# Sorting the experts by size on the chip, and converting six of the eight experts' weights piece by piece between the expert blocks

## The chip, the cores and the metric

The kernel runs on one core of a Trainium2 chip. The metric is the time of one execution in microseconds, measured on the device; the median of several runs counts. The core's engines are TensorE (PE in the profile; PEld is its weight load), VectorE (DVE), ScalarE (ACT), GpSimd (POOL) and SyncE (SP, which here only issues DMAs; SPq is its queue).

## The reference

x is (8, 512, 256) in float32, so 4096 tokens of 256 numbers. Every product is computed in split form, three float16 products for one float32 product.

```python
xn = layernorm(x)
# s: gated linear recurrence over the 512 steps of each of 8 sequences
q, v = xn @ Wq, xn @ Wv
state[t] = sigmoid(beta) * state[t-1] + v[t]
s = (layernorm(q * state) * ln_g + ln_b) * silu(xn @ Wg) @ Wo
# g: mixture of 8 experts, two per token
logits = xn @ router.T
top_vals, top_idx = top_k(logits, 2);  gates = softmax(top_vals)
for e in range(8):
    a, b = split(xn @ w_in[e].T)          # 512 hidden each
    acc += gates[:, e] * ((silu(a) * b) @ w_out[e].T)
out = x + s * silu(acc + bias)
```

## The kernel before

**Stages.** First x is loaded, normalized, transposed and routed in 8 chunks (one sequence of 512 tokens each). VectorE works out for each token its two experts, its slot in each expert's region of `slots_dram`, and the table of blocks. Then the recurrence runs over the 8 chunks (`recur` on each engine). Beside it GpSimd scatters the 4096 rows twice into `slots_dram` (64 indirect DMAs, line 534; in chunk c after its rstd, 9, 9, 8, 8, 8, 8 of them from chunk 0 on, after 14 at the start). Then comes the expert stage: 39 blocks. The slots of each expert are cut into pairs of 128-row tiles (up to 32 blocks of 256 rows) and odd tiles (7 blocks of 128 rows, run as blocks 28 to 34). Blocks 0 and 1 are written out, blocks 2 to 25 are a loop over two blocks. At the end the summed expert outputs are read back, passed through SiLU, multiplied by s and added to x.

**The recurrence, chunk by chunk.** VectorE scans (line 1008, two instructions), converts weights (line 1017), multiplies by q (line 1021, which waits for TensorE's projection into `bankB`), multiplies by the gate and splits the chunk before (lines 1060, 1066), takes statistics (1038, 1045) and hands mean and variance over (1049, 1050). GpSimd makes rstd from them (498, 499), then does that chunk's scatters; its queue is in order, so the rstd of the next chunk stands behind them. ScalarE rescales (737), TensorE transposes, projects and so on. The order is that of the code on every engine.

**The weights.** The expert weights (8 experts, 3072 columns each per partition) come as float32 and are kept as two float16 parts, `w_hi` and `w_lo`. They are loaded in 24 pieces of 1024 columns through four buffers `wst`. ScalarE writes the high part (line 709, `convert_w`), VectorE the low part (line 1017), which frees the buffer (`w_lo_ready`), and SP loads the next (line 358). Before, four pieces are converted in each of six chunks of the recurrence, and TensorE's first expert block waits for all 24.

**A block of the expert stage.** SP loads the slots and transposes them by DMA (line 405) one block ahead. TensorE computes the hidden layer into `bankA` and `bankB` (24 matmuls each) and then the outputs of the block before into `bankD` (24). ScalarE takes SiLU (759) and the high part (764), VectorE the product (1086) and the low part (1090), each twice per block, and VectorE the gating (1107). GpSimd prepares gates and targets (559 to 597) and adds the two tiles to `y_dram` with indirect DMAs (608); each block's wait for those of the block before to have landed. Two loads of x for the end (line 433) go out after every second block from block 2 on, seven in all; they are written into the part of `work` that also holds `wst`.

**Names.** `n_pair` and `n_odd` are the pairs and odd tiles of each expert, `blk_row` and `blk_off` a block's first row and its weights' offset, `blk_e` its expert. `step(...)` on VectorE is an instruction with a wait for its own end behind it. `FIRST_ONE` is 28, the first odd block.

## Time and profile before

| | |
|---|---|
| median of 3 runs | 490.76 us (490.18 to 490.99) |
| the profiled execution | 489.02 us, its span 487.3 us |
| mean granted TensorE clock over the span | 0.956 |
| TensorE matmul busy | 408.5 us, 84% of the span |
| VectorE, ScalarE, GpSimd busy | 300.3, 215.1 and 286.4 us |
| chain that ended last | PE 58%, DVE 15%, issue 9%, POOL 7%, DMA 7%, ACT 3% |

The span goes from the first to the last instruction of the core. The chain that ended last is followed back from the last instruction, at each step to what released it; "issue" is time in which an engine waited for nothing that the profile shows.

### The profile page before, as it was taken

How to read it: one execution, taken by the hardware profiler on the slowest of the kernel's cores; microseconds unless marked ns; L12 is line 12 of the kernel's file. 1: busy time of each engine (PE TensorE's matmuls, PEld its weight loads, DVE VectorE, ACT ScalarE, POOL GpSimd, SP SyncE). 2: the span in 40 equal slices, each digit the busy share in tenths (PEclk: the TensorE clock that was granted, in tenths of full speed). 3: DMA queues.
4: the chain of work that ended last, by engine and by line, in shares of the span. 5: the costliest groups of instructions: out<-in, count | busy, mean ns of one | idle time of the engine just before them, and what ended most of it. 6: DMA issues, size and time to landing. Idle time of an engine off the chain costs nothing.

```text
span 487.3 us, 11896 instructions
## 1 busy us (share of the span) xinstructions
PE 408.5 (84%) x3304; PEld 324.8 (67%) x3305; DVE 300.3 (62%) x602; ACT 215.1 (44%) x340; POOL 286.4 (59%) x504
## 2 busy tenths in 40 slices
PE   1757784999986999999999999999999999899000
PEld 1544352665653898888888888888888755788000
DVE  4898999999985355454554545464554544444056
ACT  3882363787756554334343434333342333332051
POOL 4725777678870325675775666666575743366532
PEclk9999899899999999999999999999999999999655
DMA  8893274567963259888766655666655455663498
GB/s 259 277 350 133 98 253 132 191 236 256 318 212 86 56 77 191 189 169 140 128 99 115 87 108 87 109 96 109 104 81 87 64 99 93 119 65 34 86 333 356
DMA packets 90810, 74.07 MB, mean 152 GB/s; under 512 B 52880, under 2 KB 82576, under 8 KB 90768
## 3 DMA queue, kind: packets, MB, share of 16 engines
q1 hardware_dynamic: 75824, 54.86, 41.9%
q0 software_dynamic: 13296, 17.83, 21.8%
q10 hardware_dynamic: 1664, 1.06, 0.7%
q8 instruction: 13, 0.21, 0.2%
q14 instruction: 13, 0.11, 0.1%
HBM read 40.00 MB, written 28.74 MB: 141 GB/s over the span
## 4 chain that ended last, share of the span: by engine, by line
PE 58%; DVE 15%; issue 9%; POOL 7%; DMA 7%; ACT 3%; SPq 1%; DVEq 0%; POOLq 0%; ACTq 0%
PE bankA L1181 19%; PE bankB L1181 19%; PE bankD L1181 17%; POOL slots_dram L534 4%; DMA w_raw<-x_in 2%; PE bankC L1181 2%; DMA y_dram<-rows_raw 2%; DVE w_raw L1017 1%; POOL stat L498 1%; DVE work L1008 1%; DVE bn L1038 1%; DMA w_raw<-y_dram 1%; DVE w_raw L1166 1%; DVE bn L833 1%; DVE work L1021 1%
## 5 line engine op out<-in xcount | busy, mean ns | idle before, releaser
L608 POOL DMA_INDIRECT y_dram<-rows_raw x64 | 103.3, 1614 | 27.2 <-issue 27.2
L1181 PE MATMUL bankD<-w_raw,rows_raw 128*128 x852 | 99.5, 273 | 0.3 <-DVE rows_raw L1090 0.3
L534 POOL DMA_INDIRECT slots_dram<-rows_raw,pos_i x64 | 74.2, 1159 | 30.9 <-issue 20.0
L1181 PEld LDWEIGHTS bankD<-w_raw,rows_raw 128*128 128x128 f16 x852 | 83.0, 98 | 12.0 <-issue 0.7
L1181 PE MATMUL bankA<-rows_raw,w_raw 128*128 128x256 f16 x768 | 89.1, 273 | 1.3 <-DMA rows_raw<-rows_raw 1.3
L1181 PE MATMUL bankB<-rows_raw,w_raw 128*128 128x256 f16 x768 | 89.1, 273 | 0.0
L1181 PEld LDWEIGHTS bankA<-rows_raw,w_raw 128*128 x768 | 74.8, 98 | 10.6 <-issue 1.9
L1181 PEld LDWEIGHTS bankB<-rows_raw,w_raw 128*128 x768 | 75.1, 98 | 8.7
L1090 DVE TENSOR_TENSOR rows_raw<-rows_raw 128x512 f16<-128x512 f32 x64 | 44.4, 694 | 45.5 <-ACT rows_raw L764 45.5
L1086 DVE SCALAR_TENSOR_TENSOR rows_raw<-rows_raw,bankA 128x512 f32<-128x512 f32 x32 | 22.0, 687 | 77.4 <-ACT rows_raw L759 75.1
L764 ACT ACTIVATE rows_raw<-rows_raw 128x512 f16<-128x512 f32 x64 | 40.3, 630 | 51.5 <-DVE rows_raw L1086 51.5
L759 ACT ACTIVATE rows_raw<-bankA 128x512 f32<-128x512 f32 x32 | 19.1, 596 | 96.1 <-PE bankA L1181 80.0
L605 POOL TENSOR_TENSOR rows_raw<-spare 128x1 f32<-128x1 f32 x32 | 6.2, 193 | 50.0 <-DVE rows_raw L1107 23.2
L1107 DVE TENSOR_SCALAR rows_raw<-bankD,rows_raw 128x256 f32<-128x256 f32 x64 | 27.9, 478 | 3.2 <-PE bankD L1181 3.2
L559 POOL TENSOR_TENSOR rows_raw<-rows_raw,blk_e 128x2 f32<-128x2 f32 x32 | 19.8, 618 | 13.9 <-DMA rows_raw<-slots_dram 13.9
L1017 DVE SCALAR_TENSOR_TENSOR w_raw<-work,w_raw 128x1024 f32 (+1 forms) x24 | 27.6, 1212 | 0.0
L1071 DVE TENSOR_TENSOR rows_raw<-rows_raw 128x512 f16<-128x512 f32 (+1 forms) x39 | 24.8, 636 | 3.2 <-ACT rows_raw L748 3.2
L737 ACT ACTIVATE work<-bankD,stat 128x256 f32<-128x256 f32 x32 | 15.4, 562 | 23.8 <-POOL stat L499 23.8
L498 POOL TENSOR_TENSOR stat<-stat,neg_half 128x4 f32<-128x4 f32 x16 | 16.9, 1054 | 15.0 <-DVE stat L1050 14.3
L608 POOL DMA_INDIRECT y_dram<-work,rows_raw x7 | 11.6, 1658 | 23.4 <-DMA y_dram<-work,rows_raw 12.9
L1181 PE MATMUL bankC<-wat_hi,work 128*128 128x256 f16 x128 | 23.8, 284 | 1.1 <-ACT work L730 1.1
L748 ACT ACTIVATE rows_raw<-rows_raw 128x512 f16<-128x512 f32 (+1 forms) x39 | 22.5, 577 | 2.6 <-DMA rows_raw<-slots_dram 2.6
(182 smaller groups left out, 638.7 us busy)
## 6 DMA issues: line engine op xcount, KB each, us to landing
work<-w_exp_in SPq DMA_DIRECT2D x24, 512.0 KB, 5.3
rows_raw<-slots_dram SPq DMA_DIRECT2D x32, 256.0 KB
w_raw<-x_in SPq DMA_DIRECT2D x9, 512.0 KB, 4.5
y_dram<-bias_in SPq DMA_DIRECT2D x4, 1024.0 KB, 12.3
w_raw<-y_dram SPq DMA_DIRECT2D x8, 512.0 KB, 7.2
out<-w_raw SPq DMA_DIRECT2D x8, 512.0 KB, 4.9
work<-x_in SPq DMA_DIRECT2D x7, 512.0 KB
slots_dram<-fill SPq DMA_DIRECT2D x9, 260.0 KB, 6.0
```

The source lines that it names most:

```text
L498: step(pool.tensor_tensor(stat[i][:, 1, :], stat[i][:, 0, :], neg_half[:, :], ALU.pow))
L534: pool.indirect_dma_start(out=slots_dram, out_offset=bass.IndirectOffsetOnAxis(slot, 0), in_=row, in_offset=None, bounds_check=SLOTS - 1, ...
L559: pool.tensor_tensor(is_first[i][:, :], meta_in[i][:, :, 0], e_b, ALU.subtract)\
L608: pool.indirect_dma_start(out=y_dram, out_offset=bass.IndirectOffsetOnAxis(to, 0), in_=ones_y[:, b - FIRST_ONE, :] if ones else ys[i][:, s ...
L748: act.activation(split16[i][:, 0:units(b), 0, :], slot_in[i][:, 0:units(b), :], ACT.Copy)\
L764: act.activation(g_hi[i][:, 2 * j:2 * j + 2, 0:n], g32[j][:, :, 0:n], ACT.Copy)\
L1017: dve.scalar_tensor_tensor(w_lo[:, piece], wst[:, i % STAGES, :], WSCALE, w_hi[:, piece], ALU.mult, ALU.subtract).then_inc(w_lo_ready, 1)
L1071: dve.tensor_tensor(split16[i][:, 0:units(b), 1, :], slot_in[i][:, 0:units(b), :], split16[i][:, 0:units(b), 0, :], ALU.subtract).then_inc ...
L1086: dve.scalar_tensor_tensor(g32[j][:, :, 0:n], sil[j][:, :, 0:n], 1.0 / WSCALE, AB[j][:, :, BLOCK:BLOCK + n], ALU.mult, ALU.mult).then_inc( ...
L1090: dve.tensor_tensor(g_lo[i][:, 2 * j:2 * j + 2, 0:n], g32[j][:, :, 0:n], g_hi[i][:, 2 * j:2 * j + 2, 0:n], ALU.subtract).then_inc(g_split, 1)
L1107: last = dve.tensor_scalar(ones_y[:, n, :] if ones else ys[i][:, s, :], bankD[:, i, s * D:s * D + D], gates[:, s:s + 1], None, ALU.mult)
L1181: last = pe.matmul(out_ap, lhsT, rhs, start=(n == 0), stop=(n == len(todo) - 1))
```

## The change

The experts are sorted by their number of pairs, largest first, on VectorE (`sort_experts`, called in the first chunk of the recurrence), and the table of blocks is built over the sorted experts. The weights are loaded in the sorted order: a piece's place in DRAM is read from a table (`piece_of`), a third of an expert per piece. Six pieces (two experts) are converted in the recurrence, one per chunk: ScalarE in chunks 1 to 6, VectorE in chunks 2 to 7. The other 18 are converted one per block, in blocks 0 to 17. TensorE waits for three pieces before block 0 and for b + 3 before block b. The loads of x are split: three after blocks 2 to 4, four after blocks 26 to 29. The loops of VectorE, ScalarE and SP over the chunks, and SP's over blocks 2 to 17, are written out; the expert blocks 2 to 17 are a loop over four blocks on VectorE and ScalarE.

```diff
-W_CHUNKS = CH - 2
-PIECES = 4
-PIECE = E * EW // (W_CHUNKS * PIECES)
+PER_EXPERT = 3
+PIECE = EW // PER_EXPERT
+PIECES = E * PER_EXPERT
+EARLY_PIECES = 6
+LAST_PIECE_BLOCK = PIECES - EARLY_PIECES
+X_FIRST = 3
+ID_STEP = 4096
...
 # SP
-            load_w(0)
+            def load_w(p):
+                if p >= STAGES:
+                    sp.wait_ge(w_lo_ready, p + 1 - STAGES)
+                piece = sp.value_load(piece_of[0:1, p:p + 1], min_val=0, max_val=PIECES - 1)
+                sp.dma_start(wst[:, p % STAGES, :], w_exp_v[:, bass.ds(piece, 1), :].rearrange(
+                    "p a w -> p (a w)")).then_inc(wst_loaded[p % STAGES], 16)
...
-            for c in range(1, 3):
-                load_w(c)
-
-            with sp.Fori(3, W_CHUNKS) as c:
-                load_w(c)
+            sp.wait_ge(experts_sorted, 1)
+            for p in range(STAGES):
+                load_w(p)
...
+            for p in range(STAGES, EARLY_PIECES + 3):
+                load_w(p)
 
             sp.wait_ge(pads_filled, 16 * (E + 1))
             sp.wait_ge(rows_scattered, 16 * N_SCATTERS)
...
+            for b in range(2, LAST_PIECE_BLOCK):
+                next_slots(b, b % 2)
+                if b + EARLY_PIECES + 1 < PIECES:
+                    load_w(b + EARLY_PIECES + 1)
+                if b == 2:
+                    sp.wait_ge(o_ps, CH)
+                if b - 2 < X_FIRST:
+                    load_x(b - 2)
...
+            with sp.Fori(LAST_PIECE_BLOCK, FIRST_ONE - 3, 2) as b:
+                next_slots(b, 0)
+                next_slots(b + 1, 1)
+            sp.wait_ge(w_lo_ready, PIECES)
             for b in range(FIRST_ONE - 2, BLOCKS):
                 next_slots(b, b % 2)
+                if X_FIRST <= b - FIRST_ONE + 2 + X_FIRST < X_EARLY:
+                    load_x(b - FIRST_ONE + 2 + X_FIRST)
 # ScalarE, in the recurrence
-                for i in range(PIECES if convert else 0):
-                    convert_w(c, i)
+                if 1 <= c <= EARLY_PIECES:
+                    convert_w(c - 1, (c - 1) % STAGES)
 # ScalarE, in the expert stage
+            with act.Fori(2, LAST_PIECE_BLOCK - 3, STAGES) as b:
+                for j in range(STAGES):
+                    halves(b + j, j % 2, 2)
+                    convert_w(b + (EARLY_PIECES + j), j)
 # VectorE
+            def sort_experts():
+                step(dve.scalar_tensor_tensor(key[:, :], n_pair[:, 0:E], float(E), ids, ALU.mult, ALU.subtract))
+                step(dve.tensor_tensor(beats[:, :, :], in_columns(key[:, :]), in_rows(key[:, :]), ALU.is_gt))
+                step(dve.tensor_reduce(rank[:, :], beats[:, :, :], AX.X, ALU.add))
+                step(dve.tensor_tensor(is_rank[:, :, :], in_rows(ids), in_columns(rank[:, :]), ALU.is_equal))
+                step(dve.tensor_tensor(by_rank[:, :, :], is_rank[:, :, :], in_columns(ids), ALU.mult))
+                step(dve.tensor_reduce(order[:, 0:E], by_rank[:, :, :], AX.X, ALU.add))
...
+            def low_w(p, stage):
+                dve.wait_ge(w_hi_ready, p + 1)
+                piece = bass.ds(p * PIECE, PIECE)
+                dve.scalar_tensor_tensor(w_lo[:, piece], wst[:, stage, :], WSCALE, w_hi[:, piece],
+                                         ALU.mult, ALU.subtract).then_inc(w_lo_ready, 1)
...
-                for i in range(PIECES if convert else 0):
-                    dve.wait_ge(w_hi_ready, (c - 1) * PIECES + (i + 1))
-                    piece = bass.ds(((c - 1) * PIECES + i) * PIECE, PIECE)
-                    dve.scalar_tensor_tensor(w_lo[:, piece], wst[:, i % STAGES, :], WSCALE, w_hi[:, piece],
-                                             ALU.mult, ALU.subtract).then_inc(w_lo_ready, 1)
+                if 2 <= c <= EARLY_PIECES + 1:
+                    low_w(c - 2, (c - 2) % STAGES)
...
+            with dve.Fori(2, LAST_PIECE_BLOCK - 3, STAGES) as b:
+                for j in range(STAGES):
+                    halves(b + j, j % 2)
+                    gate_y(b + (j - 1), 1 - j % 2, False)
+                    low_w(b + (EARLY_PIECES + j), j)
 # TensorE
-                pe.wait_ge(w_lo_ready, W_CHUNKS * PIECES)
+                pe.wait_ge(w_lo_ready, PER_EXPERT)
...
-            with pe.Fori(2, FIRST_ONE - 3, 2) as b:
+            with pe.Fori(2, LAST_PIECE_BLOCK + 3, 2) as b:
+                for j in range(2):
+                    pe.wait_ge(w_lo_ready, b + (j + PER_EXPERT))
+                    one_block(b + j, j)
+            pe.wait_ge(w_lo_ready, PIECES)
+            with pe.Fori(LAST_PIECE_BLOCK + 4, FIRST_ONE - 3, 2) as b:
                 one_block(b, 0)
                 one_block(b + 1, 1)
```

In the listings below a row is the line of the kernel, the operation, the tile written, those read, and the size; xN stands for N in a row. An ISA row sets or waits. Lines of the changed kernel differ: 1059 is the conversion (1017 before), 1079 the product with q (1021), 1069 the scan (1008), 414 the transposes (405), 394 the load of slots (385), 367 the load of weights (358), 434 that of x (433).

On VectorE, first chunk of the recurrence, between the counting of blocks and the product with q (`bankB`) there stood:

```order
L938 SCALAR_TENSOR_TENSOR w_raw<-w_raw 128x8
L940 SCALAR_TENSOR_TENSOR w_raw<-w_raw 128x8
L942 SCALAR_TENSOR_TENSOR w_raw<-w_raw 128x8
L1021 SCALAR_TENSOR_TENSOR work<-bankB,work 128x1024
L898 TENSOR_TENSOR w_raw<-w_raw 128x128
```

In the changed kernel the sorting (lines 960 to 974) stands behind the first of these rows, ahead of the two scans and the product:

```order
L960 SCALAR_TENSOR_TENSOR w_raw<-w_raw 128x8
L961 TENSOR_TENSOR w_raw<-w_raw 128x64
L962 TENSOR_REDUCE w_raw<-w_raw 128x8
L963 TENSOR_TENSOR w_raw<-w_raw 128x64
L964 TENSOR_TENSOR w_raw<-w_raw 128x64
L965 TENSOR_REDUCE w_raw<-w_raw 128x8
L966 SCALAR_TENSOR_TENSOR piece_of<-w_raw 1x24
L971 TENSOR_TENSOR w_raw<-w_raw 128x64
L972 TENSOR_TENSOR w_raw<-w_raw 128x64
L973 TENSOR_REDUCE w_raw<-w_raw 128x8
L974 TENSOR_REDUCE w_raw<-w_raw 128x8
L987 SCALAR_TENSOR_TENSOR w_raw<-w_raw 128x8
```

So 11 instructions more stand ahead of the product with q, the positions of the second half of the rows, and the first chunk's statistics.

On VectorE, one of the chunks 2 to 6, from the scan to the product with q, before:

```order
L1008 SCALAR_TENSOR_TENSOR work<-cols,bankA 128x512 x2
L1015 ISA
L1017 ISA
L1017 SCALAR_TENSOR_TENSOR w_raw<-work,w_raw 128x1024
L1015 REGISTER_ALU
L1017 ISA
L1017 SCALAR_TENSOR_TENSOR w_raw<-work,w_raw 128x1024
L1015 REGISTER_ALU
L1017 ISA
L1017 SCALAR_TENSOR_TENSOR w_raw<-work,w_raw 128x1024
```

A fourth conversion and then the product follow there. The same chunk now:

```order
L1069 SCALAR_TENSOR_TENSOR work<-cols,bankA 128x512 x2
L1059 SCALAR_TENSOR_TENSOR w_raw<-work,w_raw 128x1024
L1079 SCALAR_TENSOR_TENSOR work<-bankB,work 128x1024
L1118 TENSOR_TENSOR work<-work 128x512 x2
L1124 TENSOR_TENSOR work<-work 128x512 x2
```

One conversion is left between the scans and the product.

On SP, from the transposes of block 2 on, before:

```order
L405 DMA_TRANSPOSE rows_raw<-rows_raw 128x4x128 x2
L384 TENSOR_LOAD blk_row
L384 ISA x2
L385 ISA
L385 DMA rows_raw<-slots_dram 128x2x256
L405 DMA_TRANSPOSE rows_raw<-rows_raw 128x4x128 x2
L391 TENSOR_LOAD blk_row
L391 ISA x2
L392 ISA
L392 DMA rows_raw<-slots_dram 128x2x4
L433 DMA work<-x_in 128x1024 x2
```

And in the changed kernel:

```order
L414 DMA_TRANSPOSE rows_raw<-rows_raw 128x4x128 x2
L366 TENSOR_LOAD piece_of
L366 ISA x2
L367 ISA
L367 DMA work<-w_exp_in 128x1024
L434 DMA work<-x_in 128x1024
L393 TENSOR_LOAD blk_row
L393 ISA x2
L394 ISA
L394 DMA rows_raw<-slots_dram 128x2x256
L414 DMA_TRANSPOSE rows_raw<-rows_raw 128x4x128 x2
```

A load of weights and a load of x (behind a wait for the last output projection) now stand ahead of the slots of block 5 and the transposes of block 3.

## Rows read from the trace of the kernel before

**Rows 1.** Chain that ended last: start us, us, what, merged over like pieces

```profile
144.70 3.34 DMA slots_dram<-rows_raw,pos_i
...
161.85 2.62 PE bankA L1181 x24
...
186.42 2.62 PE bankA L1181 x24
...
194.28 2.62 PE bankA L1181 x24
```

**Rows 2.** Order of time, GpSimd, recurrence: start, us, instruction [idle before <-released by]

```profile
58.61 1.05 POOL L498 TENSOR_TENSOR stat<-stat,neg_half 128x4 f32<-128x4 f32 x1
...
73.73 1.05 POOL L498 TENSOR_TENSOR stat<-stat,neg_half 128x4 f32<-128x4 f32 x1
...
90.63 1.04 POOL L498 TENSOR_TENSOR stat<-stat,neg_half 128x4 f32<-128x4 f32 x1 [1.93 <-DVE stat L1050]
...
95.81 1.98 POOL L534 DMA_INDIRECT slots_dram<-rows_raw,pos_i  x1 [0.30 <-issue]
98.09 0.97 POOL L534 DMA_INDIRECT slots_dram<-rows_raw,pos_i  x1 [0.30 <-issue]
...
104.60 1.06 POOL L498 TENSOR_TENSOR stat<-stat,neg_half 128x4 f32<-128x4 f32 x1
...
118.69 1.06 POOL L498 TENSOR_TENSOR stat<-stat,neg_half 128x4 f32<-128x4 f32 x1
...
132.76 1.24 POOL L498 TENSOR_TENSOR stat<-stat,neg_half 128x4 f32<-128x4 f32 x1
...
145.69 1.05 POOL L498 TENSOR_TENSOR stat<-stat,neg_half 128x4 f32<-128x4 f32 x1
```

**Rows 3.** Order of time, VectorE and ScalarE, recurrence

```profile
44.60 0.29 DVE L875 TENSOR_TENSOR w_raw<-w_raw 128x128 f32<-128x128 f32 x1
...
51.79 0.17 DVE L938 SCALAR_TENSOR_TENSOR w_raw<-w_raw 128x8 f32<-128x8 f32 x1
52.00 0.17 DVE L940 TENSOR_TENSOR_SCAN w_raw<-w_raw 128x8 f32<-128x8 f32 x1
...
57.74 0.16 DVE L1050 TENSOR_SCALAR stat<-mv 128x4 f32<-128x4 f32 x1
...
70.31 0.15 DVE L1050 TENSOR_SCALAR stat<-mv 128x4 f32<-128x4 f32 x1
...
93.46 4.60 DVE L1017 SCALAR_TENSOR_TENSOR w_raw<-work,w_raw 128x1024 f32 x4
...
101.88 3.89 ACT L709 ACTIVATE w_raw<-work 128x1024 f32 x4
```

**Rows 4.** Order of time, TensorE, recurrence: query projections of two chunks

```profile
93.63 0.59 PE L1181 MATMUL bankB<-xs_raw,wat_hi 128*128 x2
...
105.77 0.59 PE L1181 MATMUL bankB<-xs_raw,wat_hi 128*128 x2
```

**Rows 5.** Order of time, four engines, expert stage

```profile
178.89 2.52 SPq L405 DMA_TRANSPOSE rows_raw<-rows_raw  x2
...
197.02 0.60 ACT L759 ACTIVATE rows_raw<-bankA 128x512 f32<-128x512 f32 x1 [3.29 <-PE bankA L1181]
...
197.65 0.69 DVE L1086 SCALAR_TENSOR_TENSOR rows_raw<-rows_raw,bankA 128x512 f32<-128x512 f32 x1 [2.35 <-ACT rows_raw L759]
...
205.65 1.59 POOL L608 DMA_INDIRECT y_dram<-rows_raw  x1 [0.52 <-issue]
...
212.90 0.19 POOL L605 TENSOR_TENSOR rows_raw<-spare 128x1 f32<-128x1 f32 x1 [1.31 <-DMA y_dram<-rows_raw]
...
222.26 1.60 POOL L608 DMA_INDIRECT y_dram<-rows_raw  x1 [0.52 <-issue]
```

**Rows 6.** Stretches: busy per engine, granted clock, DMA share, GB/s

```profile
core 0: us, PE busy (x) PEld busy (x) DVE busy (x) ACT busy (x) POOL busy (x), PEclk, DMA share, GB/s
181.00:189.00 8.00, 8.00 (x76) 6.96 (x74) 4.09 (x7) 2.94 (x5) 3.75 (x12) 1.00 1.24 212
162.00:382.00 220.00, 220.00 (x2017) 197.16 (x2016) 114.44 (x195) 86.95 (x148) 137.38 (x300) 1.00 0.66 112
```

113 lines of the change are left out of this document (64 added, 49 removed).

## The prediction, made before the changed kernel ran

> **What bounds the kernel now.** I read the chain of waits first, then one engine at a time in order of time, then the busy time in stretches.
>
> The kernel has three stretches. From about 162 us to 382 us TensorE runs without a gap at a granted clock of 1.00, the higher level of 2.4 GHz [rows 6]; nothing that an engine beside it does there costs anything until TensorE has to wait for it. The end behind that stretch (the blocks of one tile, the last blocks, the sum and the store) keeps its instructions. So the change can gain only before 162 us, and lose after it.
>
> Before 162 us the chain runs, from about 90 us on, through GpSimd: its scatters of token rows stand on the chain until the last one (issued at 144.70, landed at 148.04), then the loads of the first slots, and at 161.85 the first expert block begins [rows 1]. GpSimd's queue holds, for each chunk, the four small instructions for rstd and then eight or nine scatters. The starts of L498 give its pace: 58.61, 73.73, 90.63, 104.60, 118.69, 132.76, 145.69 [rows 2]. The three chunks from 90.63 to 132.76 take 42.13, so 14.04 each. GpSimd waits there once, 1.93 us before 90.63, for VectorE's variance [rows 2]; otherwise it is its own bound. Its scatters don't all cost the same: one takes 0.97 us at 98.09, but 1.98 us at 95.81, and the latter lies in the 4.60 us of VectorE's four conversions at 93.46 [rows 2, 3]. At 98.09, when the conversions have just ended and their loads are still in flight, the scatter is fast again, so I take VectorE and not the DMA traffic for the cause. The price per chunk: the scatters between two L498 take 14.04 us with four conversions in the way, and 12.93 us in the last such chunk (132.76 to 145.69) [rows 2], over which only the tail of the conversions falls.
>
> TensorE has its own floor in this stretch: from the query projection of one chunk (93.63) to that of the next (105.77) it runs without a gap, 12.14 us [rows 4].
>
> **The change part by part.**
>
> Sorting the experts puts 11 VectorE instructions ahead of the product and of the positions of the second half. A step of 8 elements per partition costs 0.21 us from start to start (51.79 to 52.00), one of 128 elements is busy for 0.29 us, so 0.33 with the same gap [rows 3]. Most of the new ones have 64 elements and waits behind them: between the two, taken as 0.26; one has 8 elements, two are not waited for. 8 x 0.26 + 0.21 + 2 x 0.15 = 2.6 us. (All at the lower bound 2.3, all at the upper 3.6.) They delay the first variance, whose last instruction starts at 57.74 and ends at 57.90, to 60.5. GpSimd's first rstd started at 58.61, behind 14 scatters [rows 2, 3], and now waits: **+1.9 us** on GpSimd.
>
> The conversions: before, VectorE has four of them in each of six chunks; now one in each of six (chunks 2 to 7, none in chunk 1). For GpSimd, chunk 1 took 73.73 - 58.61 = 15.12; I take off 1.6 for the conversions that no longer hold its scatters (two scatters of nearly 2 us in place of two of 0.97, less a little), which gives rstd 1 at 60.5 + 13.5 = 74.0, where it was. The next chunk worked until 90.63 - 1.93 = 88.70; with one conversion instead of four I take off 1.1, so it is done at 87.9. VectorE decides now: variance 1, whose last instruction started at 70.31, comes 0.5 later (behind GpSimd's later rstd 0, through the rescaling, the transposes and the statistics), the table of blocks has six instructions more at 0.12 to 0.26 (+1.4), and three conversions less in chunk 2 save 3 x 4.60/4 = 3.4 us [rows 3]. So rstd 2 moves from 90.63 to 90.63 + 0.6 + 1.4 - 3.4 = 89.2: **-1.4 us**.
>
> From there three chunks run at GpSimd's pace again. With one conversion per chunk the row that is nearest is the chunk of 12.93 us; 12.9 each, against 14.04, is 3 x 1.1 = **-3.4 us**. The bounds are nothing (the scatters stay slow, rival 1) and TensorE's 12.14, which would give 3 x 1.9 = 5.7. The last chunk changes nothing: its conversions hardly met it. One conversion in VectorE's chunk 7 lies ahead of a wait for TensorE and costs nothing; the path there goes over the scatters' landing and the slots [rows 1].
>
> Here the Trainium skill speaks against my reading of the scatters. SBUF — State Buffer, section Who interferes with whom, says that a VectorE instruction with two SBUF inputs holds up only GpSimd instructions that read SBUF, and infers that writing DMA descriptors needs the other interface, so that such an instruction would not slow a scatter. By that rule the slow scatters have another cause and the -3.4 falls away; this case's rows (1.98 against 0.97 us) point the other way.
>
> In the expert stage ScalarE gets one more conversion per block (3.89 us for four in the trace [rows 3], so 1.0 each) and VectorE one of 1.15, for 18 pieces. In a block of 7.86 us (186.42 to 194.28 [rows 1]) ScalarE stands idle 3.29 us before its first SiLU (197.02) and VectorE 2.35 us before its first product (197.65) [rows 5]. The new instructions are written behind the last use of each engine's block, so they fall into these gaps: 0 us, as long as the piece has landed. If the gap were gone, each would cost up to 1.2 us per block. The weight loads: 15 more (blocks 2 to 16), 512 KB each, one block ahead and more of their conversion. DMA is busy 0.66 of the stretch 162 to 382, and reached 1.24 where two loads of x are in flight (181 to 189), without a wait of TensorE [rows 6]. TensorE's own new waits (block b for b + 3 pieces) are met three blocks early: VectorE has converted b + 6 by the end of block b.
>
> One place is tight. SP used to issue the transposes of block 3 from 178.89 on [rows 5], ahead of any load of x; now a weight load, the wait for the last output projection (which ends where block 2 begins, one block ahead of 186.42, so about 178.5) and a load of x stand ahead of them. They are needed at 186.4, when block 3 begins, 7.5 us after 178.89 [rows 1]. I put **+0.3 us** here, between nothing and 1.5. The loads of x 3 to 6 come at blocks 26 to 29, one per block, and end long before the sum needs them: 0.
>
> Sum: -1.4 - 3.4 + 0.3 = -4.5 us (the +1.9 is inside the -1.4). The profiled execution takes 489.02 (span 487.3), so 484.5; it lies 1.74 below the median of the runs, so that the median goes from 490.76 to **486.3 us**. The bounds of the terms alone (sort 2.3 to 3.6, pace 12.14 to 13.3, block 3 nothing to 1.5) give 483.5 to 488.5.
>
> **The rivals.**
>
> 1. The scatters stay slow for a reason that isn't VectorE. Then rstd 1 comes at 60.5 + 15.1 = 75.6 and rstd 2 at 75.6 + 14.96 = 90.6, where it was, and all chunks keep 14.04: 490.8 plus 0.3. For it: the page above. Against it: the scatters at 95.81 and 98.09. Chance 0.07.
>
> 2. TensorE becomes the bound of the recurrence, because single conversions fall beside the rstd instructions and delay no scatter: 12.14 per chunk, 486.3 - 2.3 = 484.0. For it: the variance is ready about 2.5 us before GpSimd comes to it, so the conversion lies about there. Chance 0.12.
>
> 3. The chain of scatter-adds falls behind in the expert stage. Each block's needs the one before it landed; with loads of x in flight two pairs after 205.65 the next starts at 222.26, 8.3 us for each over a block's 7.86, and at 212.90 GpSimd is seen behind a wait of 1.31 us for the landing [rows 5]. So a block under load adds 0.44 of lag. Lag is paid only when VectorE's gating waits for the scatters of two blocks back: they may take 15.7 us and take 7.2 (205.65 to 212.90), so from 8.5 us of lag on. 15 blocks at 0.44 give 6.6; with conversions beside the scatters' start it could pass 8.5. If it bites: 1 to 3 us, so 488.5. Chance 0.07.
>
> 4. Slower: the DMA engines become the bound of the 15 blocks with loads. Per block they are busy 0.66 x 7.86 = 5.2 us, so 2.7 are spare. The stretch from 181 to 189 has the base of 5.3 and 1.24 x 8 = 9.9 in all, so two loads of x and their neighbours took 4.6, or 2.3 each: below 2.7, but not far. From 2.7 us a load the transposes come late in each block. At 3.3 a load: 15 x 0.6 = 9 us lost, 486.3 + 9 = 495. Chance 0.09.
>
> **How the numbers follow.** My forecast (484.8 to 488.4) has 0.65; with rival 2 and rival 3 nine tenths of what is left ends faster too. A change of 0.2%, about 1 us, is what a measurement of this kernel can tell from none. Faster by over 0.2%: 0.65 + 0.12 + 0.06 = 0.83. Within: 0.07 + 0.01 = 0.08. Slower: 0.09. The range 483.3 to 490.0 leaves out rivals 1 and 4 and a little of rival 2, under 2 in 10.
>
> **What would show each step.** In the changed profile: GpSimd's L498 of the recurrence first at about 60.5 and with a wait for VectorE, then at 74, 89.2, 102, 115, 128; scatters of about 1.9 us nearly gone; the first block of TensorE at about 157.4; TensorE busy all of the 220 us behind it; the idle times of ScalarE and VectorE in a block down to about 2.2 and 1.2. It is wrong if the paces stay at 14 us, if TensorE shows a wait for a transpose or for a conversion in blocks 2 to 17, or if the time from the first block to the end grows.

## The result and the profile after

| | before | changed |
|---|---|---|
| median | 490.61 us (490.18 to 490.99, 4 runs) | 483.22 us (482.23 to 484.36, 4 runs) |
| ratio of the times, 95% interval | | 0.985 (0.9826 to 0.9875) |
| profiled execution, span | 489.02, 487.3 us | 484.36, 482.6 us |
| start of the first expert block | 161.85 us | 153.27 us |
| from there to the end of the span | 325.5 us | 329.3 us |

Faster, by 7.4 us where 4.5 were forecast; 483.22 lies just below the range. The lead at the first expert block is even larger, 8.6 us, and 3.9 us of it are gone again at the end of this profiled execution. Two more sets of the changed kernel gave 481.78 and 482.22 us (below).

GpSimd in order of time, the starts of the recurrence's rstd (L511 is what L498 was; answers to [rows 2]):

```profile
60.66 1.04 POOL L511 TENSOR_TENSOR stat<-stat,neg_half 128x4 f32<-128x4 f32 x1 [1.91 <-DVE stat L1108]
...
74.01 1.06 POOL L511 TENSOR_TENSOR stat<-stat,neg_half 128x4 f32<-128x4 f32 x1
...
88.89 1.04 POOL L511 TENSOR_TENSOR stat<-stat,neg_half 128x4 f32<-128x4 f32 x1 [0.16 <-DVE stat L1108]
...
102.48 1.04 POOL L511 TENSOR_TENSOR stat<-stat,neg_half 128x4 f32<-128x4 f32 x1 [0.66 <-DVE stat L1108]
...
115.24 1.05 POOL L511 TENSOR_TENSOR stat<-stat,neg_half 128x4 f32<-128x4 f32 x1
...
127.39 1.06 POOL L511 TENSOR_TENSOR stat<-stat,neg_half 128x4 f32<-128x4 f32 x1
...
139.52 1.06 POOL L511 TENSOR_TENSOR stat<-stat,neg_half 128x4 f32<-128x4 f32 x1
```

The first start waits 1.91 us for VectorE's variance. The distances are 13.35, 14.88, 13.59, 12.76, 12.15 and 12.13 us; before they were 15.12, 16.90, 13.97, 14.09, 14.07 and 12.93 [rows 2].

VectorE in order of time (answers to [rows 3]): the sort lies between the first two rows, then one conversion (L1059) of a later chunk and the product behind it:

```profile
52.15 0.17 DVE L960 SCALAR_TENSOR_TENSOR w_raw<-w_raw 128x8 f32<-128x8 f32 x1
...
54.62 0.17 DVE L987 TENSOR_TENSOR_SCAN w_raw<-w_raw 128x8 f32<-128x8 f32 x1
...
117.19 1.20 DVE L1059 SCALAR_TENSOR_TENSOR w_raw<-work,w_raw 128x1024 f16<-128x1024 f32 x1
...
120.15 1.23 DVE L1079 SCALAR_TENSOR_TENSOR work<-bankB,work 128x1024 f32<-128x1024 f32 x1 [1.76 <-PE bankB L1243]
```

VectorE waits 1.76 us for TensorE behind its conversion, and TensorE has no gap through these two chunks:

```profile
115.20:139.50 24.30, 24.30 (x155) 15.94 (x153) 18.72 (x39) 14.79 (x22) 18.77 (x21) 1.00 0.38 132
```

The first three numbers are the length of the stretch, TensorE's busy time in it and its count of instructions. So TensorE bounds these chunks, at the 12.14 us that its own gapless stretch showed before [rows 4].

The chain of waits, from the last scatter to the first expert blocks, and in the tail (answers to [rows 1]):

```profile
138.53 2.48 DMA slots_dram<-rows_raw,pos_i
142.97 3.15 DMA rows_raw<-slots_dram
146.68 0.77 ACT work L709
...
150.46 2.81 PE bankC L1243 x24
153.27 2.62 PE bankA L1243 x24
...
395.22 5.06 DMA rows_raw<-rows_raw
...
410.45 6.42 DMA y_dram<-work,rows_raw
...
428.36 3.78 DMA y_dram<-work,rows_raw
...
454.54 3.90 DMA y_dram<-rows_raw
```

This splits the 8.6 us. The last scatter is issued 6.17 us earlier (138.53 against 144.70), and lands after 2.48 us in place of 3.34, which gives 0.86. The third part is the output projection behind the last chunk, 24 matmuls, which took 2.81 us here and 4.41 before (157.44 to 161.85), 1.60. In the profile before, its stretch from 157 to 161.5 us has a mean granted clock of 0.62, partly the lower level (1.2 GHz); the stretch from 150 to 153.3 of the changed kernel has 1.00 (2.4 GHz). The stretch before (the clock is the third number from the end):

```profile
157.00:161.50 4.50, 4.06 (x23) 3.04 (x24) 2.14 (x12) 1.21 (x3) 1.20 (x2) 0.62 0.50 112
```

Busy time in stretches of the changed kernel (answers to [rows 6]):

```profile
core 0: us, PE busy (x) PEld busy (x) DVE busy (x) ACT busy (x) POOL busy (x), PEclk, DMA share, GB/s
150.00:153.30 3.30, 2.84 (x26) 2.82 (x27) 2.17 (x12) 0.41 (x1) 0.91 (x1) 1.00 0.39 80
174.00:222.00 48.00, 47.84 (x437) 42.19 (x436) 31.29 (x48) 23.74 (x37) 32.24 (x65) 1.00 1.14 197
222.00:374.00 152.00, 152.00 (x1395) 136.24 (x1394) 90.56 (x146) 67.20 (x109) 107.77 (x212) 1.00 0.79 134
```

The expert stage holds: TensorE is busy 47.84 of 48 us with the DMA share up at 1.14, and all of the 152 us behind. But each block's scatter-adds into y now start later. I call lag the time from the end of the gating on VectorE (L1162, L1107 before) to the block's first scatter-add on GpSimd: 3.4 to 6 us here in blocks 1 to 26; before, it is 0.8 to 3.4 us, and only 0.8 to 1.8 from block 8 on. Two groups of the page show the same:

```profile
L572 POOL TENSOR_TENSOR rows_raw<-rows_raw,blk_e 128x2 f32<-128x2 f32 x32 | 29.4, 919 | 5.9 <-DMA rows_raw<-slots_dram 5.9
...
L1162 DVE TENSOR_SCALAR rows_raw<-bankD,rows_raw 128x256 f32<-128x256 f32 x64 | 27.9, 478 | 5.3 <-DMA y_dram<-rows_raw 3.1
```

GpSimd's destination rows take 919 ns in the mean, 618 before. From 410 us on the tail's chain in this profile is almost wholly scatter-adds and their landings, and the gating waits for them, 1.26 us at 427.07 and more at 445.40:

```profile
445.40 0.88 DVE L1162 TENSOR_SCALAR rows_raw<-bankD,rows_raw 128x256 f32<-128x256 f32 x2 [3.08 <-DMA y_dram<-rows_raw]
```

The last scatter-add is issued 4.6 us ahead of before (454.54, 459.09 before), where the lead had been 8.1 us when the blocks of one tile began (374.81 against 382.92). In neither profile of before nor in the two repeats of the changed kernel below does the gating wait for a scatter-add: there TensorE's blocks are the chain up to the last ones.

### The profile page after: what moved, and what is told of

It is laid out like the page before. It is cut to its first block, busy times and chain, and to the rows that moved or that the text cites. A ratio compares the mean times of both kernels' runs of the same rounds, so it can differ in the third digit from the quotient of the medians.

```text
span 482.6 us, 11903 instructions
## 1 busy us (share of the span) xinstructions
PE 409.0 (85%) x3304; PEld 325.9 (68%) x3305; DVE 304.8 (63%) x619; ACT 215.3 (45%) x340; POOL 288.7 (60%) x504
## 4 chain that ended last, share of the span: by engine, by line
PE 57%; DMA 12%; DVE 12%; issue 9%; POOL 6%; ACT 2%; SPq 1%; DVEq 0%; POOLq 0%; ACTq 0%
PE bankA L1243 18%; PE bankB L1243 18%; PE bankD L1243 15%; DMA y_dram<-work,rows_raw 4%; POOL slots_dram L547 3%; DMA y_dram<-rows_raw 3%; PE bankC L1243 3%; DMA w_raw<-x_in 2%; PE bankD L1342 1%; POOL stat L511 1%; DMA rows_raw<-rows_raw 1%; DMA w_raw<-y_dram 1%; DVE work L1069 1%; DVE bn L852 1%; DVE w_raw L1228 1%
## 5 line engine op out<-in xcount | busy, mean ns | idle before, releaser
L621 POOL DMA_INDIRECT y_dram<-rows_raw x64 | 109.3, 1707 | 24.6 <-issue 23.6
L547 POOL DMA_INDIRECT slots_dram<-rows_raw,pos_i x64 | 67.3, 1052 | 31.2 <-issue 20.6
L618 POOL TENSOR_TENSOR rows_raw<-spare 128x1 f32<-128x1 f32 x32 | 9.3, 289 | 51.0 <-DMA y_dram<-rows_raw 39.4
L572 POOL TENSOR_TENSOR rows_raw<-rows_raw,blk_e 128x2 f32<-128x2 f32 x32 | 29.4, 919 | 5.9 <-DMA rows_raw<-slots_dram 5.9
L1162 DVE TENSOR_SCALAR rows_raw<-bankD,rows_raw 128x256 f32<-128x256 f32 x64 | 27.9, 478 | 5.3 <-DMA y_dram<-rows_raw 3.1
L1059 DVE SCALAR_TENSOR_TENSOR w_raw<-work,w_raw 128x1024 f32 (+1 forms) x24 | 29.1, 1210 | 0.7 <-ACT w_raw L723 0.7
L511 POOL TENSOR_TENSOR stat<-stat,neg_half 128x4 f32<-128x4 f32 x16 | 16.7, 1041 | 15.0 <-DVE stat L1108 14.3
L723 ACT ACTIVATE w_raw<-work 128x1024 f32 (+1 forms) x24 | 25.0, 1042 | 0.0
```

What stands on the lines that cost most here:

```text
L547: pool.indirect_dma_start(out=slots_dram, out_offset=bass.IndirectOffsetOnAxis(slot, 0), in_=row, in_offset=None, bounds_check=SLOTS - 1, ...
L572: pool.tensor_tensor(is_first[i][:, :], meta_in[i][:, :, 0], e_b, ALU.subtract)\
L621: pool.indirect_dma_start(out=y_dram, out_offset=bass.IndirectOffsetOnAxis(to, 0), in_=ones_y[:, b - FIRST_ONE, :] if ones else ys[i][:, s ...
L723: act.activation(w_hi[:, bass.ds(p * PIECE, PIECE)], wst[:, stage, :], ACT.Copy, scale=WSCALE)\
L1059: dve.scalar_tensor_tensor(w_lo[:, piece], wst[:, stage, :], WSCALE, w_hi[:, piece], ALU.mult, ALU.subtract).then_inc(w_lo_ready, 1)
L1162: last = dve.tensor_scalar(ones_y[:, n, :] if ones else ys[i][:, s, :], bankD[:, i, s * D:s * D + D], gates[:, s:s + 1], None, ALU.mult)
```

## The experiments

Ratios are to the kernel before, run on the same chip in turns, with 95% intervals; the times of one set shouldn't be compared closer than about 1 us with those of another.

**1. The changed kernel again, twice.**

> The changed kernel a second time, for another profile and for a comparison on the chip of the next three. Open are two parts of its gain that I had not forecast: the first block began 8.6 us earlier instead of 4.8, of which 1.6 us is a projection ahead of it that ran at a granted clock of 0.5 before and at 1.0 after; and 3.4 us were given back behind block 28. If the clock part is chance, this profile may show the projection slow again (4.4 us instead of 2.8); if it belongs to the change, it is fast again. If the loss behind block 28 belongs to the change, the scatter-adds are again about 6 us behind the gating at block 27 and bind the end; if it was chance, the lag is under 3 us. Time 482 to 484.5 us.

> The changed kernel again, beside the next one on the same chip. Theory 1, the output projection at the higher clock belongs to its shorter wait of TensorE ahead of it: the 24 matmuls take 2.81 us again, and the time is 481.5 to 483.5. Theory 2, chance: 4.4 now and then.

481.78 us, ratio 0.9818 (0.9778 to 0.9857), and 482.22 us, 0.9824 (0.9799 to 0.9848). The projection took 2.81 us in both. Starts of rstd at 74.48, 90.50 and 103.55 in the first, then 12.12 to 12.15 apart. The first block began at 153.55 and 152.18, but the rest of the span took 325.65 us in one and 328.12 in the other. So what lies behind the first block varies by 3.7 us among three executions of one kernel, and the first profile was its worst. The lag was 2.5 to 5.3 us in blocks 1 to 26 of the first repeat and 1.9 to 4.0 in the second, and the second took longer behind its first block. In the second repeat TensorE waits at the heads of blocks 3 and 4 for transposes:

```profile
177.22 2.79 PE L1243 MATMUL bankA<-rows_raw,w_raw 128*128 128x256 f16 x24 [0.51 <-DMA rows_raw<-rows_raw]
...
186.39 2.79 PE L1243 MATMUL bankA<-rows_raw,w_raw 128*128 128x256 f16 x24 [1.14 <-DMA rows_raw<-rows_raw]
```

1.65 us in sum; 0.9 in the other repeat, about 0.2 in the first profile (TensorE is busy 47.84 of 48 us from 174 to 222). The recurrence varies too, up to rstd 2 (88.89, 90.50 and, in the second repeat, 89.04).

**2. Before again.**

> The kernel before, once more, for a second profile of it. In the first the output projection behind the last chunk (157.44 to 161.85, 24 matmuls) ran at a granted clock of 0.66 and took 4.41 us, 2.81 in every other profile so far. Theory 1: chance; it takes 2.8 here, and the first expert block is at 160.2. Theory 2: it belongs to that kernel (TensorE idles longer in each chunk there), and the 4.4 comes again, which would be 1.6 us of the gain. The pace of the chunks stays 14.0.

489.76 us, ratio 1.0005 (0.9979 to 1.0031). The slow projection came again, 4.42 us from 157.32 on. TensorE in order of time, the transposes and the first matmul behind them:

```profile
155.11 1.06 PE L1280 MATMUL bankD<-ident,work 128*128 128x128 f32 x8 [2.30 <-ACT work L696]
157.32 0.40 PE L1181 MATMUL bankC<-wat_hi,work 128*128 128x256 f16 x1 [1.15 <-ACT work L730]
```

and in the changed kernel's first profile:

```profile
148.25 1.06 PE L1342 MATMUL bankD<-ident,work 128*128 128x128 f32 x8 [0.41 <-ACT work L709]
150.46 0.30 PE L1243 MATMUL bankC<-wat_hi,work 128*128 128x256 f16 x1 [1.15 <-ACT work L744]
```

The waits of TensorE ahead of those transposes differ: 2.51 and 2.30 us in the two profiles of before, 0.25 to 0.52 in the three of the changed kernel. Experiments 3, 5 and 6 have more on it.

**3. What the sort costs.** Before, with the sort alone, its results unused:

```diff
@@ def count_blocks():
                                               ALU.mult, ALU.add))
+                sort_experts()
                 step(dve.tensor_tensor_scan(pair_end[:, :], ...
```

> The kernel before with the 11 instructions of the sorting added at their place in the first chunk, their results unused, the list of blocks and the conversions as before. My theory: VectorE has no idle time up to the variance of chunk 2, so the 2.6 us show in full there; the first rstd moves from 58.6 to 60.6, the third from 90.6 to about 93.2, and the kernel takes 2.6 us more than before (0.5%). Rival: GpSimd's wait of 1.9 us ahead of the third rstd takes it up, and the kernel takes 0 to 0.7 us more.

493.08 us, ratio 1.0046 (1.0016 to 1.0077): 2.7 us slower than before on the same chip (490.38). GpSimd's first and third rstd:

```profile
60.68 1.04 POOL L502 TENSOR_TENSOR stat<-stat,neg_half 128x4 f32<-128x4 f32 x1 [1.91 <-DVE stat L1082]
...
94.45 1.04 POOL L502 TENSOR_TENSOR stat<-stat,neg_half 128x4 f32<-128x4 f32 x1 [3.32 <-DVE stat L1082]
```

With four conversions per chunk in place nothing in the recurrence absorbs the sort: rstd 2 comes 3.8 us later than in the profile before. The first block comes only 2.4 us later (164.22), because the output projection took 2.81 us in this profile, after a wait of TensorE of 2.22 us ahead of the transposes. So the fast projection can also come at the old pace of 14.09 us.

**4. VectorE or the DMA traffic?** Before, without 20 of its 24 weight loads, all conversions kept (they convert the first four pieces again and again):

```diff
@@ sync engine
-            for c in range(1, 3):
-                load_w(c)
-            with sp.Fori(3, W_CHUNKS) as c:
-                load_w(c)
@@ convert_w
-                act.wait_ge(wst_loaded[i % STAGES], c * (PIECES // STAGES * 16) + (i // STAGES * 16 + 16))
+                act.wait_ge(wst_loaded[i % STAGES], 16)
```

> The kernel before with 20 of its 24 weight loads left out (the first four pieces are converted six times over, so the expert weights are wrong); VectorE and ScalarE convert as before. The pads are filled earlier, too. Theory 1, VectorE's conversions hold up GpSimd's scatters: scatters that lie in a group of four conversions still take 1.7 to 2.0 us, the chunks still take 14.0 us, and the first block starts at most 1 us earlier (through a faster landing of the last scatter). Theory 2, the DMA traffic of the loads does: all scatters take about 1.0 to 1.3 us, the chunks 12.8 us and the kernel is 3 to 5 us faster.

489.91 us, ratio 0.9995 (0.9961 to 1.0028). VectorE's conversions, and GpSimd's scatters beside them and behind them:

```profile
108.13 4.60 DVE L1012 SCALAR_TENSOR_TENSOR w_raw<-work,w_raw 128x1024 f32 x4
...
110.47 1.96 POOL L529 DMA_INDIRECT slots_dram<-rows_raw,pos_i  x1 [0.30 <-issue]
112.74 0.97 POOL L529 DMA_INDIRECT slots_dram<-rows_raw,pos_i  x1 [0.30 <-issue]
```

No weight load is in flight, the scatters are as slow, and the last chunks are 13.98, 13.44, 14.09 and 14.15 us apart. The last scatter lands after 2.58 us, against 3.34 before. That looks like the price of the weight loads, but isn't shown to be: before, the last weight load is issued at 123.9, more than 20 us ahead of the last scatter, the DMA share during the landing is 0.25 (0.29 here), and the next kernel keeps all loads and lands after 2.55. Why it takes 3.34 before stays open. The counterpart cuts VectorE's conversions from 1024 to 8 elements in chunks 3 to 6 and keeps ScalarE's and the loads (and every block reads the first expert's weights):

```diff
-            with dve.Fori(2, W_CHUNKS + 1, 1) as c:
-                recur(c)
+            recur(2)
+            with dve.Fori(3, W_CHUNKS + 1, 1) as c:
+                recur(c, size=8)
...
```

> The kernel before with VectorE's four conversions per chunk cut from 1024 to 8 elements in the chunks 3 to 6 (and every block reads the first expert's weights, so the output is another); ScalarE's conversions, the weight loads and everything else stay, and there is no sort. Theory 1, VectorE's conversions hold up GpSimd's scatters: the chunks from rstd 2 on fall from 14.0 to TensorE's 12.14, no scatter of 1.9 us from 92 us on, first expert block at about 154. Theory 2, ScalarE's conversions or the weight loads share the blame: the pace stays at 13 or above.

483.41 us, ratio 0.9854 (0.982 to 0.9887), without any of the rest of the change. Its last three starts:

```profile
119.10 1.04 POOL L498 TENSOR_TENSOR stat<-stat,neg_half 128x4 f32<-128x4 f32 x1 [0.16 <-DVE stat L1050]
...
131.24 1.04 POOL L498 TENSOR_TENSOR stat<-stat,neg_half 128x4 f32<-128x4 f32 x1 [0.16 <-DVE stat L1050]
...
143.34 1.04 POOL L498 TENSOR_TENSOR stat<-stat,neg_half 128x4 f32<-128x4 f32 x1 [0.15 <-DVE stat L1050]
```

12.14 and 12.10 us. The first block came at 157.00 and not at 154, since rstd 2 was only at 93.24, with a wait of 4.91 us for VectorE; TensorE's granted clock from 80 to 95 us was 0.66 there (0.89 before, 0.77 in the changed kernel). The pace is as theory 1 had it.

**5. Which property of the conversion?** Before, each conversion as a copy with one SBUF input (so the low halves of the weights are left out):

```diff
-                    dve.scalar_tensor_tensor(w_lo[:, piece], wst[:, i % STAGES, :], WSCALE, w_hi[:, piece],
-                                             ALU.mult, ALU.subtract).then_inc(w_lo_ready, 1)
+                    dve.tensor_copy(w_lo[:, piece], wst[:, i % STAGES, :]).then_inc(w_lo_ready, 1)
```

> The kernel before with each of VectorE's 24 conversions as a copy of the same 1024 elements from fp32 to fp16, one SBUF input in place of two (the low halves of the weights are wrong). Theory 1, two SBUF inputs are what holds up GpSimd's descriptor writing: the scatters beside the copies take 0.97 and the pace is 12.14, also where the copies last as long as before. Theory 2, any VectorE instruction with wide SBUF data does it: scatters beside them stay slow while a copy lasts, so the excess per chunk shrinks only as far as the copies are shorter than 4.6 us.

482.58 us of two runs (479.32 and 485.83), ratio 0.9841 (0.9761 to 0.9922). Four copies take 2.46 us in place of 4.60. VectorE and GpSimd:

```profile
79.89 2.46 DVE L1017 CAST w_raw<-work 128x1024 f32 x4
...
79.91 3.29 POOL L534 DMA_INDIRECT slots_dram<-rows_raw,pos_i  x1 [0.30 <-issue]
```

Theory 1 falls. This scatter takes 3.29 us, 0.83 more than the copies: it got nearly nothing done until they were over. (Beside the two-input conversions of before no scatter takes more than 1.98 us.) In the later chunks scatters take up to 1.54 us and the excess over 0.97 each is 0.7 to 0.96 per chunk, since the copies are over sooner; the pace is 12.7 to 12.8.

The same four conversions in four places of the chunk, in outline:

```diff
+                if convert: low_w(c, 0)        # behind the scan
                 ...product...
+                if convert: low_w(c, 1)
                 ...times_gate, low_p...
+                if convert: low_w(c, 2)
                 ...statistics, variance...
+                if convert: low_w(c, 3)
```

> The kernel before with the same four conversions per chunk, no longer in one row but one behind the scan, one behind the product, one ahead of the statistics and one behind the variance. It tells number from grouping. Theory 1, the time that scatters are held up is the conversions' own time beside them, wherever it lies: about 2 us excess per chunk as before, pace 14, time 490. Theory 2, a scatter is held only by a conversion that already runs when it starts, and one that starts later lets it through (as at 117.19 in the changed kernel), so four single ones cost less than a row of four: excess 0.5 to 1.3, pace 12.5 to 13.2, time 486 to 488.

499.55 us, ratio 1.0186 (1.0158 to 1.0215), 9 us slower. Both theories missed it:

```profile
90.77 1.98 POOL L498 TENSOR_TENSOR stat<-stat,neg_half 128x4 f32<-128x4 f32 x1 [1.19 <-DVE stat L1057]
...
108.09 1.98 POOL L498 TENSOR_TENSOR stat<-stat,neg_half 128x4 f32<-128x4 f32 x1 [2.83 <-DVE stat L1057]
...
124.10 1.98 POOL L498 TENSOR_TENSOR stat<-stat,neg_half 128x4 f32<-128x4 f32 x1 [1.33 <-DVE stat L1057]
```

GpSimd waits in every chunk for the variance, and the conversion behind the variance falls on L498, which takes 1.98 in place of 1.05 us. The excess of the scatters (1.1 to 2.0 us per chunk) shrank little. What delays the variance stands in the chain and on ScalarE:

```profile
109.33 3.62 DMA work<-w_exp_in
...
113.08 1.06 ACT L709 ACTIVATE w_raw<-work 128x1024 f32 x1 [2.42 <-DMA work<-w_exp_in]
```

VectorE's last conversion of a chunk now comes after the variance and frees its buffer late (107.95 to 109.17). Only then is the next piece loaded, ScalarE waits for it to convert it, and the rescaling of the next chunk stands behind that conversion in ScalarE's queue. From 90 to 160 us these loads are 21.6% of the chain. Two more conversions stand between the product and the variance, where the row of four stood ahead of VectorE's wait for TensorE. The paces are 16 to 17.6 us. So this kernel doesn't tell number from grouping: another path bounds it.

And the changed kernel's single conversion, moved from behind the scan to ahead of the statistics:

```diff
-                if 2 <= c <= EARLY_PIECES + 1:
-                    low_w(c - 2, (c - 2) % STAGES)
                 dve.wait_ge(q_ps, c + 1)
 ...
                 else:
                     place(1)
+                if 2 <= c <= EARLY_PIECES + 1:
+                    low_w(c - 2, (c - 2) % STAGES)
```

> The changed kernel with each single conversion of the chunks 2 to 7 behind the low halves of the product and ahead of the statistics, where GpSimd scatters, in place of behind the scan, where it mostly computes rstd. Theory 1, its place matters: a slow scatter of 1.3 to 1.9 us in each chunk, variance 1.2 us later, pace 12.3 to 12.8 and the first block 1 to 2 us later than 153.4. Theory 2, one conversion is covered by TensorE's 12.14 at any place: no change, 481.8.

484.98 us, ratio 0.9886 (0.9864 to 0.9908). The pace is not the reason: starts at 115.16, 127.30, 139.43, with an excess of 0.23 to 0.73 us in each of the last four chunks, where the changed kernel has 0.35 to 1.18. One conversion and the scatter beside it:

```profile
111.53 1.22 DVE L1059 SCALAR_TENSOR_TENSOR w_raw<-work,w_raw 128x1024 f16<-128x1024 f32 x1
...
111.37 1.08 POOL L547 DMA_INDIRECT slots_dram<-rows_raw,pos_i  x1 [0.30 <-issue]
```

A scatter that has begun 0.16 us before a single conversion is hardly held (1.08 us). What the kernel lost stands in its chain of waits:

```profile
138.31 5.17 DMA slots_dram<-rows_raw,pos_i
...
152.57 4.75 PE bankC L1243 x24
```

A weight load of 512 KB is issued at 137.76, since it waits for that conversion, and the last scatter beside it lands after 5.17 us in place of 2.5. Then TensorE has waited 3.34 us ahead of the transposes, and the projection takes 4.75 us: first block at 157.3.

**6. The list and the sort off the first chunks.** First the sort behind the first variance, then the list in four parts in chunks 1 to 4 as well (and two more weight loads ahead of SyncE's wait for the list), then that with the conversion in its later place:

```diff
                 if not later:
                     count(1)
-                    count_blocks()
 ...
-                if isinstance(c, int) and c == 1:
-                    list_blocks()
+                if isinstance(c, int) and c == 0:
+                    count_blocks()
+                if isinstance(c, int) and 1 <= c <= 4:
+                    list_blocks(c)
...
```

> The changed kernel with the counting and sorting of the experts moved behind the first variance on VectorE, where it no longer delays GpSimd's first rstd. Theory 1, the sort costs what it moves ahead of the first variance: rstd 0 comes at 58.7 or before, but the sort now delays chunk 1's scan, since VectorE follows with the list of blocks in that chunk, so at most 1.3 us of the 1.9 come back: 480.5 to 481.8. Theory 2, TensorE and the later chunks absorb it: no difference, 481.8.

> As the one before, and the list of blocks cut in four parts, one behind the variance of each of the chunks 1 to 4 (VectorE idles there 2 to 3 us per chunk), with two more weight loads ahead of SyncE's wait for the list. Theory 1, after the first chunk VectorE's 13 us of sorting and listing are what keeps the first three chunks above TensorE's 12.14: rstd 0 at 58.7, then 12.2 to 13.2 per chunk, so the last scatter and the first expert block come about 2.5 us sooner (151.0), and the kernel at about 479.3. Theory 2, GpSimd's own scatters set the pace of chunks 0 to 2 (15, 14.9 and 13.6 us, with eight or nine scatters each): nothing gained beyond the sort's part, 481.

> The changed kernel with the counting and sorting behind the first variance, the list of blocks in four parts behind the variances of chunks 1 to 4, and each single conversion behind the low halves of the product. Theory 1, what kept the split list from gaining were the scatters of 1.9 us beside the conversion behind the scan: rstd at 58.7, 72.4, 86.5, then 12.2 per chunk, last scatter at about 135, first block at 150, time 478.5. Theory 2, with less cover behind it the conversion ahead of the statistics delays the variance, GpSimd waits for it in chunks 2 to 4, and the list's parts delay the next scan: paces of 13 stay, time 481 to 483.

| | us | ratio | rstd 0, 1, 2, 3 at | first block |
|---|---|---|---|---|
| sort late | 482.02 | 0.9859 (0.9828 to 0.989) | 58.79, 72.42, 89.93, 102.93 | 153.04 |
| list split | 484.02 | 0.9874 (0.9846 to 0.9903) | 58.75, 72.45, 86.55, 99.14 | 152.1 |
| both and conversion later | 482.52 | 0.9839 (0.9816 to 0.9862) | 58.91, 72.58, 86.80, 99.41 | 154.2 |

The sort's delay of 1.9 us at rstd 0 costs nothing in the end: without it rstd 2 waits 2.77 us for VectorE and comes at 89.93. VectorE's list does hold chunk 1 (86.55 against 88.89), but the lead is not kept. With the list split, the chunk from 99.14 takes 13.49 us, with a slow scatter beside its single conversion:

```profile
102.27 1.20 DVE L1063 SCALAR_TENSOR_TENSOR w_raw<-work,w_raw 128x1024 f16<-128x1024 f32 x1
...
102.39 1.93 POOL L547 DMA_INDIRECT slots_dram<-rows_raw,pos_i  x1 [0.30 <-issue]
```

So a single conversion can hold a scatter as long as one of a row does, and which of the two began first decides. In seven profiles with single conversions every scatter that began inside one ended 0.83 to 0.87 us behind its end: here 0.12 us inside and 1.93 long; in the changed kernel's first profile 0.47 inside and 1.58, 0.64 and 1.40, 0.70 and 1.33. A scatter that began first took 0.97 to 1.16 us. The slow one beside the row of four in [rows 2] fits: with the four taken as equally long, that at 95.81 ends 0.88 us behind the third. A single conversion catches one scatter or none, a row of four catches two or three. In the changed kernel's last chunks the conversion starts 0.06 to 0.08 us behind the first scatter of the chunk, which takes 1.04 us, as it does in the kernel of experiment 4 without conversions beside it. In the third kernel GpSimd is its own bound at 12.59 us per chunk, above TensorE's 12.14:

```profile
112.00 1.05 POOL L511 TENSOR_TENSOR stat<-stat,neg_half 128x4 f32<-128x4 f32 x1
...
124.59 1.05 POOL L511 TENSOR_TENSOR stat<-stat,neg_half 128x4 f32<-128x4 f32 x1
...
137.18 1.06 POOL L511 TENSOR_TENSOR stat<-stat,neg_half 128x4 f32<-128x4 f32 x1
```

Each of these chunks has a scatter of 1.43 or 1.44 us. The third kernel's last scatter is issued at 136.20, 2.3 us ahead of the changed kernel's, but lands after 3.64 us, with a weight load issued at 134.51; TensorE then waits 2.48 us ahead of the transposes and its projection takes 5.31 us. None of the three beats the changed kernel beyond what these measurements can tell.

**7. Where the lead is lost behind the first block.** The late loads of x moved from blocks 26 to 29 to 20 to 23, and the changed kernel without the 15 weight loads of the expert stage (ScalarE's waits for them taken out with them):

```diff
 for b in range(LAST_PIECE_BLOCK + 2, BLOCKS):
     next_slots(b, b % 2)
-    if X_FIRST <= b - FIRST_ONE + 2 + X_FIRST < X_EARLY:
-        load_x(b - FIRST_ONE + 2 + X_FIRST)
+    if b < LAST_PIECE_BLOCK + 2 + X_EARLY - X_FIRST:
+        load_x(b - LAST_PIECE_BLOCK - 2 + X_FIRST)
```

```diff
 next_slots(b, b % 2)
-if b + EARLY_PIECES + 1 < PIECES:
-    load_w(b + EARLY_PIECES + 1)
```

> The changed kernel with its four late loads of x behind blocks 20 to 23 instead of 26 to 29; nothing else moves. Theory 1, the loads of x beside the chain of scatter-adds delay its landings just ahead of the odd blocks, where the chain has no slack to catch up: the lag at block 27 falls from 6.0 to about 3 or 4 us and the kernel gets 1 to 3 us faster than the changed one. Theory 2, the lag is that of 16 blocks with weight loads and isn't worked off anyway: the time stays within 0.5 us.

> The changed kernel without the 15 weight loads of the expert stage (pieces 9 to 23 aren't loaded; they are still converted, from what lies in the stage buffers, so six experts compute with wrong weights). It tells apart why the scatter-adds into y start 4 to 6 us behind their block in the changed kernel and 0.8 to 3.4 before. Theory 1: the loads on the DMA queues slow the landing of each scatter-add. Then without them the lag is back at 1 to 3 us in all blocks to 27, and the tail behind the last block of two tiles is some 2 us shorter, so about 480. Theory 2: it is VectorE's conversion, which starts beside GpSimd's small instructions and scatter-adds (the destination rows took 919 ns in the mean, 618 before). Then lag and time stay as they are, 481.8. Up to the first expert block nothing changes in either: about 153.4.

481.70 us, ratio 0.9813 (0.9774 to 0.9852), and 482.31 us, 0.9834 (0.9808 to 0.986): neither gains. With the loads of x earlier the lag at block 27 is 2.6 us, where the three profiles of the changed kernel have 4.8 to 6.0, and the time is the same. Without the weight loads the lag is 4.3 to 4.7 us in blocks 2 to 5, 3.4 at block 8, 2.7 at 11 and 0.95 at 23, where the changed kernel's first profile has 5.1, 3.9 and 3.4 us at blocks 8, 11 and 23. But the second repeat of the changed kernel, with all its loads, has 2.7, 2.5 and 2.3 there, so up to block 19 the loads' share in the lag isn't shown; from block 20 on it is lower than in any of the three. And the time behind the first block is 328.3 us, no less. Neither theory held: the lag went down at the end of the stage and the time stayed.

## Why the prediction was right in direction and too small

The mechanism of the gain was as forecast: fewer conversions, fewer held scatters, a shorter chunk. Three terms of the sum failed: the pace of 12.9 us behind rstd 2, "the last chunk changes nothing", and the path from the last scatter to the first block, which the prediction took as unchanged without a reason. The end, also taken as unchanged, took part of it back.

**The sort, right.** L960 to L987 is 52.15 to 54.62, so 2.47 us where 2.6 were forecast; rstd 0 at 60.66 (60.5). It costs 2.7 us by itself, as long as the four conversions stay.

**The scatters, right.** The list of blocks ends in the changed kernel at 79.4 us, and rstd 2 came at 88.89, -1.74 where -1.4 was forecast; in the repeats it came at 90.50 and 89.04, so that the mean of the three against the two profiles of before is -1.25. (The sum there added 0.6 for what the text beside it calls 0.5; nothing hangs on it.) Experiments 4 and 5 show what holds the scatters: VectorE's conversions, with the DMA traffic out of it. Rival 1 falls. The rule of the Trainium skill that spoke against it (SBUF — State Buffer, Who interferes with whom) has two sides. That a copy which may use both ports makes GpSimd "fully" block agrees with the scatter of 3.29 us beside copies of 2.46. What it says of two SBUF inputs was read too far. The scatter takes 1.96 us in place of 0.97 with no load in flight, so it is held; but it takes its positions from `pos_i`, which lies in SBUF, and if GpSimd itself reads them there, the page's own rule on instructions that read SBUF covers it. Whether that read or the writing of descriptors is held, no run here shows, so the page's inference is neither confirmed nor refuted. The small rstd instruction, which does read SBUF, takes 1.98 in place of 1.05 us beside one conversion, which agrees with the rule.

**The pace of 12.9, the wrong size.** In the first profile the sum agreed by luck: the three chunks took 38.50 in place of 42.13, -3.63 against -3.4, but as 13.59, 12.76 and 12.15, not 12.9 each. In the repeats they took 37.32 and 37.13, so -4.8 and -5.0. The settled pace is TensorE's 12.14, as in rival 2, given a chance of 0.12. The row of 12.93 us [rows 2] still held the tail of four conversions (0.95 us of excess, against 0.35 in the changed kernel), and the bound below it was the better guess for single ones. Rival 2 had them beside rstd as its condition, and that isn't how it came: the one at 117.19 starts 0.08 us behind a scatter, which takes 1.04 us. That single conversions cost so little hangs on this order. Where a scatter begins inside one, it is held (experiment 6), and a kernel in which that happens in every chunk stays at 12.59 us.

**"The last chunk changes nothing", wrong, 0.8 us.** The same pace holds for it: 12.13 against 12.93. Its conversions did meet it, by the scatters at its head.

**The path from the last scatter to the first block, taken as unchanged, wrong, 2.4 us.** The landing is 0.86 us shorter, for a reason that stays open (experiment 4). The output projection is 1.60 us shorter by its clock. I had read [rows 1] up to 161.85 without asking why 24 matmuls of the same shape took 4.41 us there; TensorE's wait ahead of the transposes before it goes from 2.5 to 0.4 us. In the 16 profiles of this study that wait parts the two: 2.30 us and more in the five with a slow projection, none to 2.22 in the eleven others. No run changes the wait alone, and the sort alone was enough for a fast projection at the old pace (experiment 3), so that the wait is the cause is argued and not shown. That the projection was fast in all three profiles of the changed kernel and slow in both of before is what makes the 1.6 us part of the gain.

**The expert stage, right in the main.** The gaps took the conversions (in block 4 ScalarE still waits 2.58 us for TensorE, VectorE 1.46 us for ScalarE, forecast about 2.2 and 1.2), TensorE stayed busy, rival 4 did not come. The term for late transposes was 0.3 in [0, 1.5] for block 3; measured 0.2, 0.9 and 1.65, at blocks 3 and 4. A wait for a transpose was one of the prediction's own signs of being wrong, and a longer time from the first block to the end was another; both came.

**The end, taken as unchanged, roughly right.** From the first block on the changed kernel took 329.3, 325.7 and 328.1 us, before 325.5 and 325.4. That is 2.3 us more in the mean. By stretch, against the mean of the two profiles of before:

| | first block to the blocks of one tile | to the last four pair blocks | to the last scatter-add | to the end |
|---|---|---|---|---|
| changed, first profile | +0.4 | +1.1 | +2.3 | +0.1 |
| first repeat | +1.1 | -0.7 | +0.2 | -0.3 |
| second repeat | +1.9 | +1.3 | +0.1 | -0.6 |

The first two columns go with TensorE's waits for transposes by DMA (0.2, 0.9 and 1.65 us in the first; 2.3, 0.3 and 2.3 us in the second, where before has 1.2 to 1.3). The third is rival 3, in one profile of three: there the lag passes the 8.5 us that the prediction had named (8.7 and 9.8 us at blocks 28 and 29; 7.1 to 7.9 in the repeats), the gating waits for landings, and the stretch is 2.3 us longer, inside the rival's 1 to 3. Up to 367 us the gating doesn't wait for it once. Why the transposes land later in some executions and why the lag differs by some 2 us between equal kernels stays open; without weight loads in the stage the end was no sooner.

In sum, by the means of the three and the two profiles, up to the last scatter -4.8 was forecast and -6.5 measured, from there to the first block nothing and -2.3, behind it +0.3 and +2.3. The spans of the three and the two profiles differ by 6.5 us (480.7 against 487.2 in the mean), the medians of the three sets by 7.4 to 8.6.
